# Moving an indirect scatter ahead of a normalisation on GpSimd, and weight transposes to the end of a pipeline's filling

## The reference

```python
q = (x @ Wq.T + bq)...; k = (x @ Wk.T + bk)...; v = (x @ Wv.T + bv)...     # 16 heads of 8
att = softmax(einsum('bhqr,bhkr->bhqk', q @ V, k @ V) / sqrt(rank))        # 512 x 512 a head
y = einsum('bhqk,bhkr->bhqr', att, v @ V) @ U.T
x = layernorm(x + y @ Wo.T + bo)
probs = softmax(x @ gate_w.T); scores, idx = top_k(probs, 2); scores /= sum(scores)
h = relu(einsum('td,ehd->teh', x, w1) + b1)
out = einsum('ted,te->td', einsum('teh,edh->ted', h, w2) + b2, combine)
x = layernorm(x + out)
```

## Time and profile before

| | us |
|---|---|
| median of 3 runs | 1260.19 |
| lowest, highest run | 1258.29, 1507.58 |
| the profiled execution | 1257.38 |
| its span, first to last instruction | 1255.6 |

### The profile page before, as it was taken

How to read it: one execution, slowest core, us unless ns; L and a number is a source line. 1 busy time by engine, 2 the same in 40 slices (tenths; PEclk the granted TensorE clock), 3 DMA queues, 4 the chain that set the end, 5 groups by cost and what they waited for, 6 DMA issues and landing times. The chain is left out here.

```text
span 1255.6 us, 24757 instructions
## 1 busy us (share of the span) xinstructions
PE 1082.8 (86%) x7711; PEld 520.5 (41%) x7711; DVE 975.3 (78%) x2117; ACT 904.2 (72%) x1177; POOL 586.5 (47%) x823
## 2 busy tenths in 40 slices
PE   3578998989889898898988999888728999999977
PEld 2222222222222222222222222222218999999952
DVE  4578888989778797887988879797146888888845
ACT  1157877778677786867878678687618999999927
POOL 1314316255271642626336263323254777777745
PEclk9989999999899998989999899899758999999989
DMA  3733133141331413223142231400012222222246
GB/s 80 235 94 90 49 101 89 54 132 42 95 92 51 126 37 106 73 67 102 43 127 69 71 97 36 122 15 19 14 51 63 69 68 69 69 69 71 66 159 257
DMA packets 105461, 104.88 MB, mean 84 GB/s; under 512 B 21608, under 2 KB 82834, under 8 KB 105376
## 3 DMA queue, kind: packets, MB, share of 16 engines
q1 hardware_dynamic: 94912, 81.88, 22.5%
q0 software_dynamic: 8448, 16.93, 4.2%
q10 hardware_dynamic: 2016, 4.98, 1.1%
HBM read 56.06 MB, written 47.39 MB: 82 GB/s over the span
## 5 line engine op out<-in xcount | busy, mean ns | idle before, releaser
L799 DVE TENSOR_REDUCE row_max<-score_ps 128x2 f32<-128x1024 f32 x512 | 618.0, 1220 | 138.9 <-PE score_ps L571 91.3
L685 ACT ACTIVATE probs<-score_ps 128x1024 f32<-128x1024 f32 x512 | 521.6, 1023 | 157.4 <-PE score_ps L553 132.6
L534 PE MATMUL av_ps<-probs,v_one 128*9 128x512 f32 x2048 | 285.2, 630 | 7.9 <-ACT probs L685 6.5
L571 PE MATMUL score_ps<-k_stack,q_stack 48*128 48x512 bf16 x1024 | 207.5, 402 | 75.2 <-ACT probs L685 57.5
L553 PE MATMUL score_ps<-q_stack,k_stack 51*128 51x512 bf16 x1024 | 205.7, 399 | 22.0 <-DVE row_max L799 15.1
L371 POOL TENSOR_TENSOR max_parts<-neg_max,zeros 32x128 bf16<-32x128 f32 x32 | 14.2, 445 | 386.9 <-ACT neg_max L623 386.9
L1096 ACT ACTIVATE w_cur<-experts 128x1156 f32 x136 | 158.5, 1167 | 37.5 <-PEq L413 17.2
L553 PEld LDWEIGHTS score_ps<-q_stack,k_stack 51*128 51x128 bf16 x1024 | 49.2, 93 | 320.4 <-issue 154.2
L1192 POOL DMA_INDIRECT y_d<-y_out,place x136 | 136.8, 1006 | 44.7 <-issue 44.7
L846 POOL DMA_INDIRECT routed_d<-rows,slot_i x128 | 125.4, 980 | 67.2 <-issue 36.9
L1053 PE MATMUL up_ps<-xt_sb,w_cur 128*128 128x128 f32 x1088 | 146.2, 278 | 0.0
(11 more groups left out here) (187 smaller groups left out, 1153.3 us busy)
## 6 DMA issues: line engine op xcount, KB each, us to landing
k_stack<-k_stack_d SPq DMA_DIRECT2D x128, 96.0 KB, 2.4
q_stack<-q_stack_d SPq DMA_DIRECT2D x128, 96.0 KB, 2.5
x_rows_sb<-routed_d SPq DMA_DIRECT2D x136, 65.0 KB
q_stack_d<-q_parts SPq DMA_DIRECT2D x32, 192.0 KB
k_stack_d<-k_parts SPq DMA_DIRECT2D x30, 192.0 KB
x_in<-L_attn_x SPq DMA_DIRECT2D x16, 256.0 KB, 3.1
q_stack_d<-q_parts SPq DMA_DIRECT2D x32, 128.0 KB
x_res<-L_attn_x SPq DMA_DIRECT2D x16, 256.0 KB, 3.1
```

What stands on the lines that cost most here:

```text
L534: last = nc.tensor.matmul(av_ps[32 * g:32 * g + V_COLS, :], v_one[n.parity][:, kb, HG * hg + g, :], probs[:, (2 * j + g // 2) % P_RING, g ...
L571: last = nc.tensor.matmul(max_bank(b, s)[:, a, :], q_stack[n.parity][at, c, g * P:(g + 1) * P], k_stack[n.parity][at, c, :], start=True, s ...
L685: nc.scalar.activation(probs[:, s % P_RING, :, :], exp_bank(b, s)[:, :, :], ACT.Exp).then_inc(S["exp_done"], 1)
L799: nc.vector.tensor_reduce(row_max[:, m // (STEPS // 2), :, m % (STEPS // 2)], max_bank(b, s)[:, :, :], AX.X, ALU.max).then_inc(S["red_done ...
```

## The change

`EXPERT_AT` was 16, 18, ... 30 and becomes 24, 25, ... 31, for PE and ACT both. On GpSimd `scatter(p2, 0, 2)` comes ahead of `split_max(b, 1)`, and the six other scatters come right behind it, ahead of the layer norm's operations, in all bodies that have a current batch; bodies 16 and 17 keep their order. In body -1 alone, `split_max(n1, 0)` moves ahead of `split_k` on GpSimd, and `max_rows(n1, 0)` moves ahead of the store of k's parts on SyncE.

```diff
-EXPERT_AT = [STEPS - 2 * (E - e) for e in range(E)]
+EXPERT_AT = [STEPS - E + e for e in range(E)]
...
-                        if cur:
-                            split_max(b, 1)
                         if prev2:
                             pool.wait_ge(S["place_out"], p2.count(1, 1))
                             pool.wait_ge(S["top_step"], p2.count(TOP_STEPS, TOP_STEPS))
                             pool.wait_ge(S["slot_step"], p2.count(SLOT_STEPS, SLOT_STEPS))
                             pool.wait_ge(S["copied"], p2.count(1, 1))
                             scatter(p2, 0, 2)
+                        if cur:
+                            split_max(b, 1)
+                        if prev2 and cur:
+                            scatter(p2, 2, 8)
                         if prev:
                             pool.wait_ge(S["mv_ready"], p1.count(QT, QT))
...
                         if proj and not is_first(b):
                             split_q(nc.gpsimd, pool, n2)
+                            if not cur:
+                                split_max(n1, 0)
                             split_k(nc.gpsimd, pool, n2)
-                        if prev2:
-                            scatter(p2, 2, 6)
-                        if nxt:
+                        if cur and nxt:
                             split_max(n1, 0)
-                        if prev2:
-                            scatter(p2, 6, 8)
+                        if prev2 and not cur:
+                            scatter(p2, 2, 8)
...
                             store_parts(sp, q_stack_d[n2.parity], q_parts, Q_PLACES)
+                        if nxt and not cur:
+                            max_rows(n1, 0)
                         if proj and not is_first(b):
...
-                        if nxt:
+                        if cur and nxt:
                             max_rows(n1, 0)
```

## The result

The changed kernel takes 1287.26 us in the median of 4 runs (1281.45 to 1287.91), the kernel before 1261.4 us in 4 runs beside it: a ratio of 1.0194, with an interval of 1.0153 to 1.0235. It is slower, by about 2%: 26 us above the kernel before, where +7 us was forecast, and 21 us above the 1266 us. The range ended at 1287 us. One of the four runs of the kernel before, 1507.58 us, stands far from the rest, and the ratio goes by the others. The profiled executions differ by 24.1 us, 1281.45 against 1257.38 us.

What follows compares the result with a forecast made beforehand. The order of work was taken to bound the kernel, with no engine full and SyncE's chain next; +2.5 (bodies 2 to 13) + 6 (14, 15) - 1.5 (filling) = +7 us gave 1264.4 profiled, 1266 us predicted, range 1234 to 1287 us.

Steps and rivals of the forecast that it cites:

- The store and the scatters together hold up the engines: Step 26 of bodies 2 to 13: k's store meeting scatters makes PE's 2.61 us wait, 2.0 us of it removable.
- A: Theory of the experiments: an unbroken run of scatters stalls the engines, wherever in the body it stands.
- The rule on the queues: DMA engines serve queues in turn, so store and scatters only share them and moving scatters removes no wait; chance 0.08.
- `shift` 3.5 us later: Layer norm, bodies 2 to 13: scatters ahead of it make `shift` end at 412.5 in place of 408.98; bounds 2.6 and 4.0.
- Scatters' pitch: GpSimd: scatters 1.28 us apart, six taking 7.36 us, read from body 16.
- ACT waits 1.7 us for `shift`, behind SyncE's chain: Bodies 2 to 13: ACT's `scale_out` waits 1.7 us, PE 2.2 us at step 17, covered by SyncE's later chain.
- Bodies 2 to 13 bound by `max_rows` at 52.8 us, +2.5 us in all: Later k's split delays `max_rows`; bodies taken as 52.9 against 52.7 us, +2.5 us for 12, bounds -12 and +14.
- The chain itself: k's split, its store, the wait, four loads, `max_rows`: 14.93 us from k's split to the next body's first scores.
- Bodies 14 and 15, +6 us: No chain hides ACT's wait for `shift`: 2.7 us in body 14, 3.9 in body 15; +6 us, from 0 to +12.
- The filling, -1.5 us, -3 to +5: Before body 0: PE's 3.56 us wait and slow matmuls go, experts end at 76.0; -1.5 us, between -3 and +5.
- The clock falls in mid-body: Rival: PE's 2.2 us idle at step 17 brings a long 1.2 GHz stretch, bodies 54.2 us and over; 1291 us, chance 0.09.
- The wait stays: Rival: step 26's wait remains, from k's store alone or following the scatters to step 12; 1284 us, chance 0.08.

Runs made afterwards that it cites:

- 3: Kernel before, with two scatters behind `split_q`, two behind `split_k` and two behind `split_max` in place of the run of four: 1262.5 us, 1.0043.
- 5: Kernel before, with row maxima loaded ahead of the stacks on SyncE and scatters only in pairs, the last pair in the next body: 1207.38 us, 0.962.
- 12: Kernel 5 with the experts' transposes at steps 24 to 31 of the filling in place of every second one from 16: 1210.75 us, 0.9594 to the kernel before.
- 4: Kernel before, with six of a batch's eight scatters in one run at the head of the next body: 1274.7 us, 1.0135.
- 7: Changed kernel with the run of six scatters right behind the layer norm's `shift` in place of ahead of it: 1330.55 us, 1.0581 to the kernel before.
- 10: Kernel 5 with scatters 2 to 8 in one run of six after the next body's fourth exp: 1271.56 us, 1.0088 to the kernel before.
- 6: Kernel before, with only SyncE's order changed, the row maxima's loads ahead of the four loads of stacks: 1258.37 us, 1.0012.
- 11: Kernel 5 with six scatters in two runs of three, behind k's split and behind the maxima's first half: 1234.49 us, 0.979 to the kernel before.
- 9: Kernel 5 with scatters 4 to 8 in one run of four after the next body's fourth exp: 1215.07 us, 0.9647 to the kernel before.

## Why the time came out at the edge, and which steps failed

- *The store and the scatters together hold up the engines*: the step that failed. Three bodies without the wait were read as "one of the two is missing". The runs show the length of the run of scatters instead: pairs beside the store stall nothing (3, 5, 12), six away from it stall 2.4 to 4.2 us (change, 4, 7, 10). The reading was also made in the wrong place: it looked at step 25, while the runs of bodies 14 and 15 stand at steps 16 to 21, and body 15's has six scatters, not four. No long wait stands there either, and that doesn't fit A alone. The changed kernel's body 14, with six, does stall (3.42 us of ACT, "remote").
- *The rule on the queues*, the Trainium skill, "DMA: Bandwidth & Descriptors", "Queues, rings and completion order". I weighed it against my reading and gave it 0.08. It was the better guide in one respect: a pair and k's store share the engines with no wait of PE, ACT or DVE (3). It doesn't account for the wait of a run at a DMA share of 0.10.
- *`shift` 3.5 us later*: 27.2 us after body 6's first exp in place of 23.8, 3.4 us. *Scatters' pitch*: 1.27 us, as said.
- *ACT waits 1.7 us for `shift`, behind SyncE's chain*: in body 6 ACT stood 4.53 us at step 15, two steps ahead of `scale_out`, and `shift` was ready when it came there. Only body 15 shows the forecast wait, 2.33 us. The new run of six was costed as GpSimd's time only, 7.36 us, and at nothing on the others; the rows of body 16 that gave its pitch come from a body without exps, where nobody could show a wait. That term had to be +3 to +4.2 us.
- *Bodies 2 to 13 bound by `max_rows` at 52.8 us, +2.5 us in all*: +12.5 us. The bodies' own work, with the run's wait in it, is longer than the chain (first scores of body 7 released by DVE). The chain itself was well read: k's split of body 6 ends at 429.8 and 14.93 us later would be 444.7, before the 445.92 of the first scores. In the kernel before, too, body 7 didn't wait for it, and taking the loads forward gave nothing (6). The term's lower bound, -12 us, doesn't follow from its parts: bodies of 51.9 us make 12 x -0.8 = -9.6 us.
- *Bodies 14 and 15, +6 us*: +9.0 us. Body 14's +4.4 us go with the run. In body 15, +4.7 us, the forecast mechanism is the one seen: `scale_out` comes 4.1 us later, 3.9 forecast. Ahead of it PE stands 2.21 us for the scores of step 16; no releaser is named, but in kernel 7, where `split_max(b, 1)` is behind the same pair of scatters, it is the load of the row maxima (1.76 us). The prediction left that out. With an early `shift` (7) body 15 takes 50.0 in place of 52.5 us.
- *The filling, -1.5 us, -3 to +5*: +5.4 us. The experts began at 56.5, as said (56.9). The term that was mis-sized is the pitch "once the clock is up": 3.14 us, not 2.27, seven times. The bound named the reason, the lower clock throughout, and was 0.4 us short.
- *The rivals*. "The clock falls in mid-body", 1291 us with 0.09, comes nearest in its time: a wait in mid-body, the lower clock behind it, and bodies of 54 us. But its wait is not the one it named. "The wait stays", 1284 us, is refuted at step 26, and near to the truth in that the wait follows the scatters.
- *The range*: the forecast's own bounds ended at 1281 us; only the rivals carried it to 1287. Added end to end the three upper bounds would have given 1259.3 + 14 + 12 + 5 = 1290 us. Three errors of one sign (the run +10 us, bodies 14 and 15 +3, the filling +7) met the 3 us that came back behind the last body. That the time ended at the range's last microsecond is luck: nothing that set that bound made the time. The forecast itself was 1266 us, for a reason that the runs refute.

## What to carry to other kernels

Cost a run of three or more indirect DMAs from GpSimd at more than its own pitch, where the other engines are at work: break it into pairs with other work or a wait between, out of the path of whatever chain GpSimd feeds. A cure that uncovers the next limit shows nothing by itself: spacing that held back k's split gave +0.4% (3), SyncE's order +0.1% (6), spacing off the chain and the order together -3.8% (5). How much of that needs the order wasn't run. The old chain, k's split at 34.1 + 14.93 = 49.0 us, would end just where these bodies of 49.2 us do, which is an estimate. When a wait is put down to two things at once because the bodies with one of them lack it, look at how many of each there are, not only at whether they are there.

## What the hardware showed that I had not expected

- A run of six indirect scatters of 128 rows each from GpSimd, 1.27 us apart, held up the exchange between PE, ACT and DVE by 2.4 to 4.2 us near its end, in four places of the body; four cost 1.0 us (head of the body) to 2.2 us (beside a store), three 0.8 to 1.0 us, two nothing. The kernel before has four and six in bodies 14 and 15 that cost 0.2 and 1.0 us, so something else must meet the run. What is held up isn't settled: the DMA engines are at a share of 0.10 to 0.23 in the changed kernel and in 10, and PE has issued its matmuls in the changed one. The Trainium skill, "DMA: Bandwidth & Descriptors", section "SWDGE vs HWDGE vs iDMA", says that GpSimd writes the descriptors of its DMAs into rings in SBUF. No run here separates that writing from the transfers.
- Behind most of these waits PE's matmuls take 0.61 in place of 0.39 us for a while, at a granted clock of 0.50. So a wait of 0.8 us can go with 2 us a body (11), and one of 1.0 us with 0.4 us where the clock stayed up (9).
- Matmuls at the durations of the lower level (0.42 and 0.61 us) stood in a stretch whose granted clock was 1.00 (12); in the changed kernel the column reads 0.50 for the same stretch. The durations tell TensorE's speed, the column alone doesn't. Why the eight late transposes never reached the faster level, while those at every second step did from about 60 us on, stays open.
